# Experts of a mixture-of-experts block: inner values computed transposed, first weights stationary and fetched per tile

## The chip, the core and the metric

The kernel runs on one core of a Trainium2 chip. The time is device microseconds from start to end of one execution. The engines named below are TensorE (PE in the rows, with its weight loads listed apart as PEld), VectorE (DVE), ScalarE (ACT), GpSimd (POOL) and SyncE (SP), which here issues nearly all plain DMAs.

## What is computed

A two-layer decoder in float32 on x of shape (8, 512, 256). The change touches only the last piece, the routed feed-forward of layer 1, where each of the 4096 rows is sent to its two best of eight experts:

```python
mu = jnp.mean(x, axis=-1, keepdims=True)
var = jnp.mean(jnp.square(x - mu), axis=-1, keepdims=True)
xn = (x - mu) * jax.lax.rsqrt(var + EPS) * gamma + beta
logits = jnp.einsum('btd,ed->bte', xn, router_w)
probs = jax.nn.softmax(logits / TEMP, axis=-1)
w, idx = jax.lax.top_k(probs, K)                     # K = 2 of E = 8
wdense = jnp.sum(jax.nn.one_hot(idx, E) * w[..., None], axis=-2)
h = jax.nn.silu(jnp.einsum('btd,edf->betf', xn, W1)) # D = 256, H = 1024
y = jnp.einsum('betf,efd->betd', h, W2)
out = jnp.einsum('bte,betd->btd', wdense, y)
return out + res
```

The kernel computes only the two chosen experts of each row, not all eight.

## The kernel before

The program is a sequence of blocks, one after the other: attention and feed-forward of layer 0, attention of layer 1, cross-attention of layer 1, then `moe` (L1946), which is `route`, `experts` and `combine`. A block ends when all engines have ended their part of it.

`route` (L1971) normalises the last two batch entries, chooses their experts, and sends the normalised rows into a DRAM area `moe_sent`, grouped by expert; each send is one indirect DMA that POOL issues (`send`, L376), and POOL ends by waiting until all have arrived (L2074). Beside this SP issues the loads of all expert weights into SBUF: for each of the eight experts `w1` (256x1024, 1 MB) at L2025 and `w2` (1024x256, 1 MB) at L2026, 16 MB in all. They signal `w_in`.

`experts` (L2178) works through 72 tiles of 128 rows. Which expert a tile belongs to (`expert_of`) and where its rows start (`row_of`) are read from SBUF into registers at run time. The loops are unrolled. For a tile i the steps are:

- SP loads the rows, `xg` (L2238, two buffers), and stores the result, `y` (L2229).
- PE transposes the rows into `X` (L2254, two transposes of 128x128), ACT copies them to `xgT` (L2301).
- PE computes H = xgT.T times w1 (L2274): stationary operand xgT (two tiles of 128x128), moving operand w1 with 512 columns, two halves in two PSUM banks, 4 matmuls. The rows of the tile lie on the partitions.
- ACT applies Silu to each half and writes `h` (L2307).
- PE transposes `h` into `HT` (L2287, eight transposes), DVE copies it in two halves to `hT` (L2333), since the second product needs the 1024 inner values on the partitions.
- PE computes Y (L2262, `down`): stationary operand hT, moving operand w2 with 256 columns, 8 matmuls; DVE copies Y to `y` (L2324).

A float32 matmul that is no transpose stands in the trace as two MATMULs and two LDWEIGHTS, and a transpose as one of each. So H of a tile is 8 MATMULs of 512 columns, Y 16 of 256 columns.

The order of PE is written out by hand in `step` (L2266): H of tile i, then `down` of tile i-1, then the transposes of the rows of tile i+1, then the eight transposes of h of tile i. Waits stand in that order too: before H for `xt_done` (rows copied), before each half of the h transposes for `h_act`, before `down` for `ht_done`. PE begins the block with a wait for all of `w_in` (L2290). SP's own order in a step is: store of tile i-1, then the row load of tile i+2 (L2235 to L2238).

`combine` (L2341) gathers the two results of each row with 64 indirect DMAs from POOL (L2365), adds them on DVE and stores.

Of the kernel before, what the change touches and what calls it, by code (L numbers as in the profile page):

```python
# [21 lines left out]
P = 128  # L22
# [3 lines left out]
DT = D // P  # L26
# [1919 lines left out]
def moe(nc, sh, w, ro, out):  # L1946
# [8 lines left out]
    with ExitStack() as ctx:  # L1955
# [5 lines left out]
        with ExitStack() as inner:  # L1961
            env2 = Env(nc, inner, "ex")
            w1 = env2.sb("w1", [P, NE, DT, FH])
            w2 = env2.sb("w2", [P, NE, FT, D])
            w_in = env2.sem("w_in")
            route(nc, sh, w, ro, w1, w2, w_in, gates, expert_of, row_of, fetch)
            experts(nc, sh, w1, w2, w_in, expert_of, row_of, ro.sent, ro.results)
# [3 lines left out]
def route(nc, sh, w, ro, w1, w2, w_in, gates, expert_of, row_of, fetch):  # L1971


    with ExitStack() as ctx:
# [45 lines left out]
        def _(sp):  # L2020
# [3 lines left out]
            for e in range(NE):  # L2024
                sp.dma_start(w1[:, e], w["w1"][e].rearrange("(t p) f -> p t f", p=P)).then_inc(w_in, 16)  # L2025
# [152 lines left out]
def experts(nc, sh, w1, w2, w_in, expert_of, row_of, sent, results):  # L2178
# [5 lines left out]
    with ExitStack() as ctx:  # L2184
# [4 lines left out]
        h = sb("h", [P, FH])  # L2189
        hT = sb("hT", [P, FT, P])  # L2190
        y_sb = sb("y", [P, 2, D])
        X = env.ps("X", [P, DT, P])
        H = [env.ps(f"H{i}", [P, 512]) for i in range(2)]
        HT = [env.ps(f"HT{i}", [P, FT // 2, P]) for i in range(2)]
        Y = [env.ps(f"Y{i}", [P, D]) for i in range(2)]
        xg_in = [sem(f"xg_in{i}") for i in range(2)]
# [4 lines left out]
        ht_full = sem("ht_full")  # L2201
        ht_done = sem("ht_done")
# [20 lines left out]
        def _(sp):  # L2223
            sp.dma_start(xg[:, 0, :], tile_rows(sp, 0)).then_inc(xg_in[0], 16)
            sp.dma_start(xg[:, 1, :], tile_rows(sp, 1)).then_inc(xg_in[1], 16)
# [5 lines left out]
            def step(pair, parity, first, more):  # L2231
                i = pair * 2 + parity
                if not first:
                    store(i - 1, 1 - parity)
                if not (isinstance(i, int) and i + 2 >= TILES):  # L2235

                    sp.wait_ge(xt_full, i + 1)
                    sp.dma_start(xg[:, parity, :], tile_rows(sp, i + 2)).then_inc(xg_in[parity], 16)  # L2238

# [6 lines left out]
        def _(pe):  # L2246
# [10 lines left out]
            def down(i, parity):  # L2257
                e = expert(i)
                pe.wait_ge(ht_done, i * 2 + 2)
                pe.wait_ge(y_done, i + 1)  # L2260
                for f in range(FT):
                    mm = pe.matmul(Y[parity][:], hT[:, f, :], w2[:, bass.ds(e, 1), f, :].rearrange("p a d -> p (a d)"),  # L2262
# [3 lines left out]
            def step(pair, parity, first, more):  # L2266
                i = pair * 2 + parity
                e = expert(i)

                pe.wait_ge(xt_done, i + 1)  # L2270
                pe.wait_ge(h_act, i * 2 + 2)
                for half in range(2):
                    for dt in range(DT):
                        mm = pe.matmul(H[half][:], xgT[:, dt, :],  # L2274
# [253 lines left out]
```

## Time and profile before

| | us |
|---|---|
| median of 3 runs | 4008.63 (4007.08 to 4018.28) |
| the profiled execution, whole | 4008.86 |
| its span, first to last instruction | 4006.7 |
| `route`, about | 3247 to 3302 |
| `experts`, first row load issued to last result copied | 3303.4 to 3885.9 |
| `combine`, to the end | 3888 to 4007 |

Over the span PE is busy 83%, DVE 57%, ACT 47%, POOL 24%. Times in the rows are microseconds from the start of the span, "x8" is a count of merged instructions, and in a timeline the second column is the length of the merged piece. A PE piece ends with the pipeline of its last MATMUL, so it overlaps the next piece by about 0.2 us; the distance between the starts of two pieces is what a piece costs when PE is fed. [...]

### The profile page before, as it was taken

What the parts mean: (1) busy time and instruction counts of PE and PEld (TensorE: products, weight loads), DVE (VectorE), ACT (ScalarE), POOL (GpSimd) and SP (SyncE); (2) the same over time, 40 slices, a digit from 0 to 9 for tenths busy, and PEclk for the clock granted to TensorE, in tenths of its full rate; (3) what the DMA queues carried; (4) which work ended last, traced back from release to release, by engine and by line L of the source; (5) the groups of instructions that cost most, each with busy time, mean ns of one, the idle gap of its engine ahead of it and who ended that gap; (6) DMA issues with size and microseconds to landing.
All of it is one profiled execution on the core that took longest, in us unless ns stands there. A gap on an engine that the chain in (4) does not pass through costs nothing. (4 is left out here: it accounts for less than half of the span.)

```text
span 4006.7 us, 74067 instructions
## 1 busy us (share of the span) xinstructions
PE 3339.5 (83%) x25632; PEld 2464.7 (62%) x25632; DVE 2300.4 (57%) x7397; ACT 1893.5 (47%) x4614; POOL 953.0 (24%) x758
## 2 busy tenths in 40 slices
PE   6888888858689589898888977999999939999970
PEld 3656565547678466665666655777777736767650
DVE  4777777758867356656666553566666642222226
ACT  4787778833342165555555534555555512121210
POOL 0000000024200376776667720001111130000014
PEclk8999999977799799999999988999999969999995
DMA  3111111010200121121212211000000051111113
GB/s 107 49 50 49 55 56 67 30 29 1 97 2 1 62 57 49 51 54 49 53 49 54 54 27 54 13 13 20 23 23 23 24 207 32 32 35 34 34 42 109
DMA packets 111257, 187.56 MB, mean 47 GB/s; under 512 B 23792, under 2 KB 66224, under 8 KB 106032
## 3 DMA queue, kind: packets, MB, share of 16 engines
q1 hardware_dynamic: 100000, 131.44, 11.4%
q0 software_dynamic: 10896, 51.39, 3.4%
q8 instruction: 216, 3.54, 0.4%
q14 instruction: 145, 1.19, 0.1%
HBM read 91.93 MB, written 57.28 MB: 37 GB/s over the span
## 5 line engine op out<-in xcount | busy, mean ns | idle before, releaser
L1064 ACT ACTIVATE a_t<-a_t,a_neg 128x512 f32<-128x512 f32 (+3 forms) x1024 | 642.6, 633 | 9.1 <-DVE a_neg L1282 8.2
L891 PE MATMUL a_T<-ident,a_t 128*128 128x128 f32 x3328 | 509.6, 287 | 125.6 <-ACT a_pT L1055 56.7
L891 PEld LDWEIGHTS a_T<-ident,a_t 128*128 128x128 f32 x3328 | 382.1, 145 | 321.2 <-issue 288.3
L1055 ACT ACTIVATE a_pT<-a_T 128x512 f32<-128x512 f32 (+3 forms) x768 | 370.1, 512 | 270.8 <-PE a_T L891 270.7
L1277 DVE CUSTOM_DVE_ANT_0 a_t<-a_A,a_decay 128x512 f32<-128x512 f32 x512 | 323.0, 687 | 99.7 <-PE a_A L856 99.5
L1277 DVE CUSTOM_DVE_ANT_0 a_t<-a_A,a_table 128x384 f32<-128x384 f32 (+3 forms) x512 | 221.0, 487 | 168.1 <-PE a_A L868 166.8
L1113 POOL TENSOR_TENSOR a_rsin<-a_rawswapped,a_sin 128x512 f32<-128x512 f32 x128 | 168.4, 1316 | 557.8 <-DMA a_rawswapped<-a_raw 535.8
L2324 DVE COPY experts_y<-experts_Y 128x256 f32<-128x256 f32 x72 | 30.6, 425 | 438.2 <-PE experts_Y L2262 438.2
L2274 PE MATMUL experts_H<-ex_w,experts_xgT 128*128 x576 | 261.2, 596 | 0.9 <-ACT experts_xgT L2301 0.6
L2262 PE MATMUL experts_Y<-ex_w,experts_hT 128*128 x1152 | 260.5, 379 | 1.0 <-DVE experts_hT L2333 1.0
L2262 PEld LDWEIGHTS experts_Y<-ex_w,experts_hT 128*128 128x128 f32 x1152 | 218.8, 190 | 61.3 <-issue 35.2
L1055 ACT ACTIVATE x_pT<-x_T 128x512 f32<-128x512 f32 (+1 forms) x320 | 178.0, 592 | 163.1 <-PE x_T L891 143.3
L1277 DVE CUSTOM_DVE_ANT_0 x_t<-x_A,x_table,x_mx 128x512 f32<-128x512 f32 x256 | 177.6, 749 | 134.2 <-PE x_A L868 133.6
L2365 POOL DMA_INDIRECT combine_got<-moe_results,moe_fetch x64 | 62.2, 973 | 628.4 <-PEq L2343 593.6
L1252 DVE COPY a_pT<-a_T 128x512 f32<-128x512 f32 (+3 forms) x256 | 148.3, 579 | 94.6 <-PE a_T L891 92.8
L2307 ACT ACTIVATE experts_h<-experts_H 128x512 f32<-128x512 f32 x144 | 86.0, 597 | 240.8 <-PE experts_H L2274 240.8
L1064 ACT ACTIVATION_READ_ACCUMULATOR a_t<-a_t,a_neg 128x1 f32 x1024 | 196.5, 192 | 0.0
L1064 ACT ACTIVATE x_t<-x_t,x_neg 128x576 f32<-128x576 f32 x256 | 194.7, 765 | 0.0
L827 PE MATMUL a_A<-a_wo,a_oT 128*128 128x256 f32 x640 | 165.1, 410 | 31.3 <-DVE a_mx L1277 22.8
L912 PEld LDWEIGHTS a_O<-a_pT,a_v 128*64 128x64 f32 x2560 | 138.1, 137 | 66.1 <-ACT a_pT L1055 41.3
L868 PE MATMUL a_A<-a_khl,a_qhl 64*128 64x128 f32 (+3 forms) x1536 | 158.0, 337 | 22.9 <-POOL a_khl L1123 20.1
L1086 POOL DMA_DIRECT2D moe_sent<-a_zeros x33 | 17.6, 539 | 659.9 <-ACT a_xT L1024 659.9
(329 smaller groups left out, 6885.7 us busy)
## 6 DMA issues: line engine op xcount, KB each, us to landing
moe_sent<-a_zeros POOLq DMA_DIRECT2D x33, 1024.0 KB, 8.2
a_rawswapped<-a_raw SPq DMA_DIRECT2D x512, 64.0 KB, 2.0
a_invrep<-a_inv_dram SPq DMA_DIRECT2D x64, 256.0 KB, 3.9
ex_w<-in_f_w_dram SPq DMA_DIRECT2D x16, 1024.0 KB
experts_xg<-moe_sent SPq DMA_DIRECT2D x72, 128.0 KB, 2.0
moe_results<-experts_y SPq DMA_DIRECT2D x72, 128.0 KB, 1.7
x_invrep<-x_inv_dram SPq DMA_DIRECT2D x32, 256.0 KB, 3.9
x_all<-in_x_dram SPq DMA_DIRECT2D x1, 4096.0 KB, 14.4
```

Of the source, the lines that this page charges most:

```text
L827: mm = pe.matmul(bank[:, 0:D], oT[:, t, qt * P:(qt + 1) * P], wo[:, t, :], start=(t == 0), stop=(t == n_o - 1))
L868: mm = pe.matmul(A[seg.bank(at)][:, 0:keys(u)], q_hl[r, gp, ql, j // 2, q], k_hl[r, gp, kl_, j // 2, 0:keys(u)], start=(n == 0), stop=(n = ...
L891: mm = pe.transpose(bank[:, kt, :], t_of(u, j, kt * P, (kt + 1) * P), sh.ident[:])
L912: mm = pe.matmul(O[pr][64 * half:64 * half + 64, q], v_sb[:, kt, col], p_tile(u, j, kt), start=(kt == 0), stop=last, skip_group_check=True)
L1055: nc.scalar.activation(to, of, ACT.Copy).then_inc(t_empty, 1)
L1064: nc.scalar.activation(t_of(u_e % U, j, 0, n), t_of(u_e % U, j, 0, n), ACT.Exp, bias=neg[:, slot, j:j + 1], scale=SCALE, accum_out=total[: ...
L1113: nc.gpsimd.tensor_tensor(rsin[:], raw_swapped[:, n % 2, :], sin[:], ALU.mult).then_inc(sin_done, 1)
L1252: nc.vector.tensor_copy(p_tile(u, 3, 0, kts), bank[:, 0:kts, :] if kts > 1 else bank[:, 0, :])\
L1277: nc.vector.tensor_tensor_reduce(t_of(s, j, 0, n), A[seg.bank(name)][:, 0:n], table[:, at:at + n], 1.0, mx1[:, slot, j:j + 1] if x1 else L ...
L2262: mm = pe.matmul(Y[parity][:], hT[:, f, :], w2[:, bass.ds(e, 1), f, :].rearrange("p a d -> p (a d)"), start=(f == 0), stop=(f == FT - 1))
L2274: mm = pe.matmul(H[half][:], xgT[:, dt, :], w1[:, bass.ds(e, 1), dt, half * 512:(half + 1) * 512] .rearrange("p a f -> p (a f)"), start=(d ...
L2307: nc.scalar.activation(h[:, half * 512:(half + 1) * 512], H[half][:], ACT.Silu).then_inc(h_act, 1)
```

## The change

The first product is turned round. `w1` becomes the stationary operand, in 16 tiles of 128x128, and `xgT` with its 128 columns the moving one, so that the 1024 inner values come out on the partitions. ACT's Silu writes them straight into `hT`, which now has two buffers. The eight transposes of h, their PSUM banks and DVE's two copies are gone. H of a tile is 16 matmuls (32 MATMULs in the trace) of 128 columns.

`w1` is no longer loaded for all experts in `route`. It has two buffers, and SP fetches the 1 MB of each tile's expert in `experts` (`weights_of`), for tile i+2 after H of tile i is done; 72 such fetches. PE waits for `w1_in` before H. `w2` is still loaded whole in `route`, and PE waits for it before the first `down`. PE's order in a step is now H of tile i, the transposes of the rows of tile i+1, `down` of tile i-1. SP's order is: row load of tile i+2, weight fetch of tile i+2, store of tile i-1.

```diff
@@ -1960,15 +1960,14 @@
         fetch = env.sb("fetch", [P, GROUPS], U32)
         with ExitStack() as inner:
             env2 = Env(nc, inner, "ex")
-            w1 = env2.sb("w1", [P, NE, DT, FH])
             w2 = env2.sb("w2", [P, NE, FT, D])
             w_in = env2.sem("w_in")
-            route(nc, sh, w, ro, w1, w2, w_in, gates, expert_of, row_of, fetch)
-            experts(nc, sh, w1, w2, w_in, expert_of, row_of, ro.sent, ro.results)
+            route(nc, sh, w, ro, w2, w_in, gates, expert_of, row_of, fetch)
+            experts(nc, sh, w["w1"], w2, w_in, expert_of, row_of, ro.sent, ro.results)
         combine(nc, sh, fetch, gates, ro.results, out)
 
 
-def route(nc, sh, w, ro, w1, w2, w_in, gates, expert_of, row_of, fetch):
+def route(nc, sh, w, ro, w2, w_in, gates, expert_of, row_of, fetch):
 
 
     with ExitStack() as ctx:
@@ -2022,7 +2021,6 @@
             sp.dma_start(beta[:], w["beta"]).then_inc(loaded, 16)
             sp.dma_start(router[:], w["router_wT"].rearrange("(t p) e -> p t e", p=P)).then_inc(loaded, 16)
             for e in range(NE):
-                sp.dma_start(w1[:, e], w["w1"][e].rearrange("(t p) f -> p t f", p=P)).then_inc(w_in, 16)
                 sp.dma_start(w2[:, e], w["w2"][e].rearrange("(t p) d -> p t d", p=P)).then_inc(w_in, 16)
 
         @block.tensor
@@ -2175,7 +2173,7 @@
             steps.link(nv.tensor_tensor(gates[:], ro.packed[:, :, NE:], total[:].to_broadcast([P, BQ, TOP]), ALU.mult))
 
 
-def experts(nc, sh, w1, w2, w_in, expert_of, row_of, sent, results):
+def experts(nc, sh, w1_dram, w2, w_in, expert_of, row_of, sent, results):
 
 
 
@@ -2186,20 +2184,18 @@
         sb, sem = env.sb, env.sem
         xg = sb("xg", [P, 2, D])
         xgT = sb("xgT", [P, DT, P])
-        h = sb("h", [P, FH])
-        hT = sb("hT", [P, FT, P])
+        w1 = sb("w1", [P, 2, DT, FH])
+        hT = sb("hT", [P, 2, FT, P])
         y_sb = sb("y", [P, 2, D])
         X = env.ps("X", [P, DT, P])
-        H = [env.ps(f"H{i}", [P, 512]) for i in range(2)]
-        HT = [env.ps(f"HT{i}", [P, FT // 2, P]) for i in range(2)]
+        H = [env.ps(f"H{i}", [P, FT // 2, P]) for i in range(2)]
         Y = [env.ps(f"Y{i}", [P, D]) for i in range(2)]
+        w1_in = [sem(f"w1_in{i}") for i in range(2)]
         xg_in = [sem(f"xg_in{i}") for i in range(2)]
         xt_full = sem("xt_full")
         xt_done = sem("xt_done")
         h_full = sem("h_full")
         h_act = sem("h_act")
-        ht_full = sem("ht_full")
-        ht_done = sem("ht_done")
         y_full = sem("y_full")
         y_done = sem("y_done")
         stored = [sem(f"stored{i}") for i in range(2)]
@@ -2221,8 +2217,14 @@
 
         @block.sync
         def _(sp):
-            sp.dma_start(xg[:, 0, :], tile_rows(sp, 0)).then_inc(xg_in[0], 16)
-            sp.dma_start(xg[:, 1, :], tile_rows(sp, 1)).then_inc(xg_in[1], 16)
+            def weights_of(i, parity):
+                e = sp.value_load(expert_of[0:1, i:i + 1], min_val=0, max_val=NE - 1)
+                sp.dma_start(w1[:, parity], w1_dram[bass.ds(e, 1)].rearrange("a (t p) f -> p (a t) f", p=P))\
+                  .then_inc(w1_in[parity], 16)
+
+            for i in range(2):
+                sp.dma_start(xg[:, i, :], tile_rows(sp, i)).then_inc(xg_in[i], 16)
+                weights_of(i, i)
 
             def store(i, parity):
                 sp.wait_ge(y_done, i + 1 + 2)
@@ -2230,12 +2232,14 @@
 
             def step(pair, parity, first, more):
                 i = pair * 2 + parity
+                if i + 2 < TILES:
+
+                    sp.wait_ge(xt_full, i + 1)
+                    sp.dma_start(xg[:, parity, :], tile_rows(sp, i + 2)).then_inc(xg_in[parity], 16)
+                    sp.wait_ge(h_full, i * 2 + 2)
+                    weights_of(i + 2, parity)
                 if not first:
                     store(i - 1, 1 - parity)
-                if not (isinstance(i, int) and i + 2 >= TILES):
-
-                    sp.wait_ge(xt_full, i + 1)
-                    sp.dma_start(xg[:, parity, :], tile_rows(sp, i + 2)).then_inc(xg_in[parity], 16)
 
             steps(sp, step)
             store(TILES - 1, 1)
@@ -2256,55 +2260,52 @@
 
             def down(i, parity):
                 e = expert(i)
-                pe.wait_ge(ht_done, i * 2 + 2)
+                pe.wait_ge(h_act, i * 2 + 2)
                 pe.wait_ge(y_done, i + 1)
                 for f in range(FT):
-                    mm = pe.matmul(Y[parity][:], hT[:, f, :], w2[:, bass.ds(e, 1), f, :].rearrange("p a d -> p (a d)"),
+                    mm = pe.matmul(Y[parity][:], hT[:, parity, f, :], w2[:, bass.ds(e, 1), f, :].rearrange("p a d -> p (a d)"),
                                    start=(f == 0), stop=(f == FT - 1))
                 mm.then_inc(y_full, 1)
 
             def step(pair, parity, first, more):
                 i = pair * 2 + parity
-                e = expert(i)
-
                 pe.wait_ge(xt_done, i + 1)
-                pe.wait_ge(h_act, i * 2 + 2)
+                pe.wait_ge(w1_in[parity], pair * 16 + 16)
                 for half in range(2):
-                    for dt in range(DT):
-                        mm = pe.matmul(H[half][:], xgT[:, dt, :],
-                                       w1[:, bass.ds(e, 1), dt, half * 512:(half + 1) * 512]
-                                       .rearrange("p a f -> p (a f)"), start=(dt == 0), stop=(dt == DT - 1))
+                    if i:
+                        pe.wait_ge(h_act, i * 2 - 1 + half)
+                    for j in range(FT // 2):
+                        f = half * (FT // 2) + j
+                        for dt in range(DT):
+                            mm = pe.matmul(H[half][:, j, :], w1[:, parity, dt, f * P:(f + 1) * P], xgT[:, dt, :],
+                                           start=(dt == 0), stop=(dt == DT - 1))
                     mm.then_inc(h_full, 1)
+                if more:
+
+                    transpose_rows(1 - parity, pair + (parity + 1))
+                if i == 1:
+                    pe.wait_ge(w_in, 16 * NE)
                 if not first:
                     down(i - 1, 1 - parity)
-                if more:
-
-                    transpose_rows(1 - parity, pair + (parity + 1))
-                for half in range(2):
-                    pe.wait_ge(h_act, i * 2 + (half + 1 + 2))
-                    for j in range(FT // 2):
-                        f = half * (FT // 2) + j
-                        mm = pe.transpose(HT[half][:, j, :], h[:, f * P:(f + 1) * P], sh.ident[:])
-                    mm.then_inc(ht_full, 1)
-
-            pe.wait_ge(w_in, 16 * 2 * NE)
+
             transpose_rows(0, 1)
             steps(pe, step)
             down(TILES - 1, 1)
 
         @block.scalar
         def _(act):
-            act.sem_inc(h_act, 2)
-
             def copy_rows(i):
                 act.wait_ge(xt_full, i + 1)
                 nc.scalar.activation(xgT[:], X[:], ACT.Copy).then_inc(xt_done, 1)
 
             def step(pair, parity, first, more):
                 i = pair * 2 + parity
+                if i >= 2:
+                    act.wait_ge(y_full, i - 1)
                 for half in range(2):
                     act.wait_ge(h_full, i * 2 + (half + 1))
-                    nc.scalar.activation(h[:, half * 512:(half + 1) * 512], H[half][:], ACT.Silu).then_inc(h_act, 1)
+                    nc.scalar.activation(hT[:, parity, half * (FT // 2):(half + 1) * (FT // 2), :], H[half][:],
+                                         ACT.Silu).then_inc(h_act, 1)
                 if more:
                     copy_rows(i + 1)
 
@@ -2328,10 +2329,6 @@
                 if not first:
 
                     result(i - 1, 1 - parity, pair + parity)
-                for half in range(2):
-                    dve.wait_ge(ht_full, i * 2 + (half + 1))
-                    nc.vector.tensor_copy(hT[:, half * (FT // 2):(half + 1) * (FT // 2), :],
-                                          HT[half][:]).then_inc(ht_done, 1)
 
             steps(dve, step)
             result(TILES - 1, 1, TILES // 2)
```

How this stands in the program of PE, for one steady step in the middle of `experts`. "ISA" is register arithmetic, TENSOR_LOAD the reading of an expert's number into a register. Before, from the end of one `down`, with the X and h transposes (L2254, L2287) and the first of the four H matmuls (L2274):

```order
L2262 ISA
L2262 MATMUL experts_Y<-ex_w,experts_hT 128x256
L2254 MATMUL experts_X<-ident,experts_xg 128x128 x2
L2287 MATMUL experts_HT<-ident,experts_h 128x128 x8
L2248 TENSOR_LOAD moe_expertof
L2248 ISA x2
L2274 ISA
L2274 MATMUL experts_H<-ex_w,experts_xgT 128x512
```

And now, with H at L2280, the X transposes at L2258 and `down` at L2266:

```order
L2266 MATMUL experts_Y<-ex_w,experts_hT 128x256
L2280 MATMUL experts_H<-experts_xgT,experts_w 128x128 x16
L2258 MATMUL experts_X<-ident,experts_xg 128x128 x2
L2252 TENSOR_LOAD moe_expertof
L2252 ISA x2
L2266 ISA
L2266 MATMUL experts_Y<-ex_w,experts_hT 128x256
L2266 ISA
```

The transposes of h are gone, H has no register work left, and the reading of the expert's number stands once in a step, behind the transposes of X.

The same for SP, one steady step. Before:

```order
L2220 TENSOR_LOAD moe_rowof
L2220 ISA x2
L2238 ISA
L2238 DMA experts_xg<-moe_sent 128x256
L2229 DMA moe_results<-experts_y 128x256
```

And now, where `experts_w` is the double buffer of w1:

```order
L2216 TENSOR_LOAD moe_rowof
L2216 ISA x2
L2238 ISA
L2238 DMA experts_xg<-moe_sent 128x256
L2221 TENSOR_LOAD moe_expertof
L2221 ISA x2
L2222 ISA
L2222 DMA experts_w<-in_f_w_dram 128x2x1024
L2231 DMA moe_results<-experts_y 128x256
```

A second register load and the 1 MB fetch stand between the row load and the store.

## Rows read from the trace of the kernel before

**Rows 1.** Stage table: us, busy of each engine, PEclk, DMA share, GB/s.

```profile
3280.00:3306.00 26.00, 0.57 (x2) 0.29 (x2) 8.67 (x17) 0.00 (x0) 11.86 (x12) 0.50 0.94 349
3562.00:3626.00 64.00, 64.00 (x274) 44.94 (x273) 13.86 (x25) 12.62 (x24) 0.00 (x0) 1.00 0.11 34
```

**Rows 2.** Timeline of one steady step: start, length, engine, line, operation, idle before.

```profile
3592.52 1.04 PE L2287 MATMUL experts_HT<-ident,experts_h 128*128 128x128 f32 x8
...
3593.39 3.60 PE L2274 MATMUL experts_H<-ex_w,experts_xgT 128*128 x8
...
3596.83 3.62 PE L2262 MATMUL experts_Y<-ex_w,experts_hT 128*128 x16
...
3597.03 0.60 ACT L2307 ACTIVATE experts_h<-experts_H 128x512 f32<-128x512 f32 x1 [1.12 <-PE experts_H L2274]
...
3600.28 0.38 PE L2254 MATMUL experts_X<-ident,experts_xg 128*128 128x128 f32 x2
...
3600.70 0.39 ACT L2301 ACTIVATE experts_xgT<-experts_X 128x256 f32<-128x256 f32 x1 [3.08 <-PE experts_X L2254]
```

**Rows 3.** Timeline, start of H of tiles 1, 2 and 71.

```profile
3313.97 3.69 PE L2274 MATMUL experts_H<-ex_w,experts_xgT 128*128 x8 [0.33 <-issue]
...
3322.05 3.60 PE L2274 MATMUL experts_H<-ex_w,experts_xgT 128*128 x8
...
3872.72 3.60 PE L2274 MATMUL experts_H<-ex_w,experts_xgT 128*128 x8
```

**Rows 4.** Weight folding of layer 0 (L1694): two timeline pieces, then its stage table.

```profile
1104.60 1.95 PE L1694 MATMUL fold_C<-fold_lowdown 128*128 128x128 f32 x16
...
1117.16 3.93 PE L1694 MATMUL fold_C<-fold_chaindown,fold_lowdown 128*128 128x128 f32 x32 [2.60 <-ACT fold_chaindown L1731]
...
1094.00:1098.00 4.00, 4.00 (x36) 3.91 (x34) 1.00 1.04 429
```

**Rows 5.** Weight load of the folding, ns min/median/max; then a cross-attention piece of 64 columns.

```profile
L1694 PEld LDWEIGHTS fold_C<-fold_lowdown x16: 187/192/192, 1104.4 to 1106.2; 128*128 128x128 f32 x16
...
3000.88 1.00 PE L791 MATMUL x_A<-x_ctxT,x_wk 128*128 128x64 f32 x8
```

**Rows 6.** PE's sequencer in the step of rows 2: ns min/median/max, first to last start.

```profile
L2248 PEldq TENSOR_LOAD <-moe_expertof x1: 447/447/447, 3593.6 to 3593.6; - x1
...
L2262 PEldq FUSED_REGOPS  x8: 46/46/46, 3594.6 to 3595.5; - x8
```

**Rows 7.** End of `route`: last send, DMA table, SP's first load; then first gathers of `combine`.

```profile
3294.24 0.96 POOL L379 DMA_INDIRECT moe_sent<-moe_router,moe_place  x1 [0.30 <-issue]
...
3300.00:3302.00 2.00, 0.00 (x0) 0.00 (x0) 0.00 (x0) 0.00 (x0) 0.00 (x0) 0.50 1.10 356
...
L2220 SPq TENSOR_LOAD <-moe_rowof x72: 262/267/505, 3302.4 to 3864.8; - x72
...
3897.68 0.95 POOL L2365 DMA_INDIRECT combine_got<-moe_results,moe_fetch  x1 [0.30 <-issue]
...
3900.50 3.45 DVE L2388 SCALAR_TENSOR_TENSOR x_all<-combine_got,moe_gates,x_all 128x256 f32<-128x256 f32 x8 [12.22 <-DMA combine_got<-moe_results,moe_fetch]
```

**Rows 8.** Timeline, start of `experts`: the first two row loads and H of tile 0.

```profile
3303.39 0.37 SPq L2224 DMA_DIRECT2D experts_xg<-moe_sent  x1
3304.55 0.36 SPq L2225 DMA_DIRECT2D experts_xg<-moe_sent  x1
...
3306.69 5.61 PE L2274 MATMUL experts_H<-ex_w,experts_xgT 128*128 x8 [0.60 <-ACT experts_xgT L2301]
```

**Rows 9.** DMA issues: what, count, KB each, median us from issue to landing.

```profile
fold_down<-in_f_w_con_dram SPq DMA_DIRECT2D x1, 1024.0 KB, 5.4
...
a_wq<-in_a_w_q_dram SPq DMA_DIRECT2D x1, 1024.0 KB, 7.7
...
moe_router<-in_f_router_row_dram SPq DMA_DIRECT2D x1, 1024.0 KB, 10.2
```

**Rows 10.** Timeline, the copy of the last result.

```profile
3885.50 0.42 DVE L2324 COPY experts_y<-experts_Y 128x256 f32<-128x256 f32 x1 [3.96 <-PE experts_Y L2262]
```

## The prediction

> **What bounds the kernel now.** I read first the stage table, because the change touches only `route` and `experts`. [...]
>
> Then the timeline of one step. The reader is to take the distance from one start to the next. The h transposes start at 3592.52, H at 3593.39, Y at 3596.83, the X transposes at 3600.28 [rows 2]. That makes 0.87 us for the h transposes (8 MATMULs, 0.109 each), 3.44 for H (8, 0.430 each), 3.45 for Y (16, 0.216 each), and 0.22 for X. Sum 7.98 us. From H of tile 2 (3322.05) to H of tile 71 (3872.72) are 69 steps [rows 3], 550.67 / 69 = 7.98 each, so this step stands for all.
>
> **Part 1: H with w1 stationary.** The columns streamed stay the same: before 8 MATMULs of 512, now 32 of 128. What changes is that each 128 columns now bring a weight load of their own, 32 a tile in place of 8. The question is how fast pairs of a full 128x128 load and a 128-column MATMUL follow each other. The old step shows such pairs only as transposes (0.109 us). The nearest row with true float32 matmuls is the folding of weights in layer 0, which has exactly the new shape: 16 MATMULs in a piece of 1.95 us, of which the last one's own length is 0.275, so 15 distances in 1.675, 0.112 us each; in a window of 4 us at clock 1.00 there are 36, 0.111 each, and this with the DMA engines at a share of 1.04 [rows 4]. A second piece, 32 in 3.93, gives (3.93 - 0.275) / 31 = 0.118 [rows 4]. The cross-attention piece with 64 columns and the same full loads, 8 in 1.00, gives about (1.00 - 0.275) / 7 = 0.104 [rows 5], so the load itself can follow the load before at about 0.104, and the columns at 0.109. I take 0.112, from the piece nearest in kind, and keep 0.109 and 0.118 as ends. H of a tile becomes 32 x 0.112 = 3.58 us (3.49 to 3.78), against 3.44.
>
> [...] What the rows show: a weight load lasts 187 to 192 ns [rows 5], and still Y's 16 pairs follow each other at 0.216 us, the time of their 256 columns alone (twice 128 at 0.109), so the loads lie beside the MATMULs. [...]
>
> **Part 2: the transposes of h are gone.** 8 x 0.109 = 0.87 us of PE a tile, wholly on the path, since PE is never idle. Steady step: 3.58 + 0.22 + 3.45 = 7.25 against 7.98, 0.73 less. There are 70 steps from H of tile 1 to H of tile 71: **51.1 us** gained (57.4 with 0.109, 37.1 with 0.118).
>
> **Part 3: what PE waits for in the new order.** Silu and the row copy cost nothing before and must still do so. ACT starts the second Silu 0.2 us after H ends (3597.03 against 3596.83) for 0.60, then copies the rows for 0.39 [rows 2]; with X transposed 0.22 after H, xgT is ready about 1.3 us after H ends, and `down` of the tile before covers 3.45. The Silu result is wanted one step later. The waits for an H bank and ACT's wait for `y_full` concern work of the tile before, done by then: nothing. The sequencer: reading the expert's number begins at 3593.6 and the register work of all eight Y matmuls is done by 3595.5 [rows 6], 1.9 us in which PE lives from its queue. Now this begins when H and X are handed over, with up to 3.8 us of work queued. I cost it at nothing; if the queue held less than that, up to 1.0 us (3593.6 to 3594.6) would show in each step. H needs no register work any more, which I count as nothing too. The two DVE copies were hidden and bring nothing.
>
> **Part 4: the fetch of w1.** It adds 72 transfers of 1 MB. One is issued when SP sees H of tile i done, after a register load (about 1.0 us from the load at 3302.4 [rows 7] to the issue at 3303.39 [rows 8]). It is needed at H of tile i+2: 0.22 + 3.45 + 3.58 + 0.22 + 3.45 = 10.9 us after H of tile i ends. So 9.8 us are there for issue to landing. Rows for 1 MB: 5.4 us alone, 7.7 in a group of loads, 10.2 behind a loaded queue [rows 9]. In steady state only 1.25 MB move in 7.25 us, 180 GB/s, where `route` moved 349 [rows 1] and the folding 429 beside dense PE work [rows 4]. I take 5.5, hidden with 4 us to spare. Behind the waiting SP instructions stands the store of tile i-1; it is ready only when `down` of i-1 ends, 3.7 us after H of i, later than the fetch's issue, and its buffer is wanted two steps later. Row loads go ahead of the fetch. Nothing.
>
> **Part 5: `route` and the start.** Half of the 16 MB leaves `route`. The DMA engines are full to 3302 (share 1.10 in 3300 to 3302), while POOL issued its last send at 3294.24 + 0.96 = 3295.2; SP's first load of `experts` is at 3302.4 [rows 7]. So the arrivals waited behind the weight loads. Without w1 the 8.4 MB less at about 0.39 MB a us are 21 us of transfer, and the loads end before the sends. In `combine` the first wait ends at 3900.50, 1.9 us after the eighth gather was issued (3897.68 + 0.95) [rows 7]. By that `route` ends at 3297.1 and SP starts at 3297.2, 5.2 earlier. Then the new start: first row load 1.0 later, 3298.2; w1 of tile 0 one load and issue later (3304.55 - 3303.39 = 1.16 [rows 8]), 3299.35; landed 5.5 later, 3304.9 (up to 3307.0 with 7.7). H of tile 0 is at the low clock for its first part: before 5.61 in place of 3.60 [rows 2, 8], 2.0 more; now 3.58 + 0.2 + 2.0 = 5.8 to its end as a piece, so 3310.6. With no `down` to cover it, PE then waits for the second Silu and the row copy, 1.2 to 1.3: H of tile 1 at 3311.9 against 3313.97 [rows 3]. **2.1 us** gained (2.9 gained at best, 0.4 lost with a slow first fetch). The wait for w2 stands before the first `down`, long met.
>
> **Part 6: the end.** Before, 3872.72 [rows 3] to the last copy at 3885.50 [rows 10] are 12.78 us: H, Y, h transposes, the wait for their copies, Y. Now 3.58 + 3.45 + 3.45 + 0.4 for the last pipeline and the semaphore = 10.9. **1.9 us** gained.
>
> **Sum.** 51.1 + 2.1 + 1.9 = 55.1. Against the profiled execution (span 4006.7, whole 4008.86, which is 0.2 from the median 4008.63): 4008.9 - 55.1 = 3953.8, so 3954.
>
> **The rivals.**
> (a) *The pair runs at the transposes' 0.109*: 57.4 + 2.9 + 2.0 = 62, time 3946. [...] Against: the folding's 0.111 to 0.112.
> (b) *The pair runs at 0.118 or a few tenths a step are lost at the sequencer*: 37.1 + 1.0 + 1.7 = 40, time 3969; with the slow first fetch 3971. For it: the longer folding piece. Against: that piece stands between waits for ACT, and the long unbroken run gives 0.111.
> [...]
> (d) *The fetch sets the pace.* From 9.8 us of landing on, two steps take 3.58 + 1.1 + the landing. At the 10.2 of the worst 1 MB row this is 7.44 a step, 0.54 gained, time 3967; slower than before only from 11.3 us on. For it: SP has one queue, with loads and stores in it. Against: the bandwidth above. [...]
> (e) *Nothing gained*: only if the transposes' 0.87 had been hidden, which PE busy 64.00 of 64 us [rows 1] excludes, or by a mixture of (b) and (d).
>
> **How the numbers follow.** Forecast 0.50 (3950 to 3960), (a) 0.20, (b) 0.18, (c) 0.03, (d) 0.06, (e) 0.03. The time is the forecast's, 3954. For the range I go down to (a) with the best start, 3944, and up to (b) and the mild form of (d), 3972; outside are (c), (e) and the bad half of (d), about 0.10, which leaves something for what I did not see. A measurement of this kernel can tell 0.3%, 12 us, from no change. Faster by more than that: the forecast, (a), (b), most of (d), 0.94. Within: (e), 0.02. Slower: (c) and the bad end of (d), 0.04.
>
> **What would show it.** In the profile after: H pieces of 32 MATMULs start to start with X in about 3.58; a step of 7.25; `experts_H` at clock 1.00; w1 landing in 5 to 8 us and PE never idle for it after the first tile; route's last arrivals some 5 us earlier; DVE busy about 1.3 us less a tile. The forecast is wrong if a gap opens before H (fetch) or before Y (sequencer), or if the distance inside H is above 0.12.

## The result

| | us |
|---|---|
| predicted | 3954 (3944 to 3972) |
| measured, median of 4 | 3950.99 (3944.79 to 3955.89) |
| before, median of its runs beside it | 4007.86 |
| ratio | 0.9861, 95% interval 0.9846 to 0.9877 |
| the profiled execution, span | 3945.3 (before 4006.7) |

The change makes the kernel 57 us faster by the medians, 1.4%. The prediction said 55.

What answers to [rows 1], the stage table of the same stretch: us, busy of PE, PEld, DVE, ACT and POOL, PEclk (the granted clock, 1.00 for full), DMA share, GB/s.

```profile
3500.00:3564.00 64.00, 64.00 (x447) 60.41 (x446) 3.82 (x9) 12.60 (x26) 0.00 (x0) 1.00 0.54 185
```

PE is as full as before and at a granted clock of 1.00, but the weight loads are now busy 60.41 of 64 us (44.94 before). DVE fell from 13.86 to 3.82, the DMA share rose from 0.11 to 0.54.

The steady step, which answers to [rows 2]:

```profile
3545.49 3.73 PE L2280 MATMUL experts_H<-experts_xgT,experts_w 128*128 128x128 f32 x32
...
3549.06 0.38 PE L2258 MATMUL experts_X<-ident,experts_xg 128*128 128x128 f32 x2
...
3549.28 3.62 PE L2266 MATMUL experts_Y<-ex_w,experts_hT 128*128 x16
...
3549.75 0.38 ACT L2299 ACTIVATE experts_xgT<-experts_X 128x256 f32<-128x256 f32 x1
3549.98 0.39 SPq L2222 DMA_DIRECT2D experts_w<-in_f_w_dram  x1
...
3552.73 3.73 PE L2280 MATMUL experts_H<-experts_xgT,experts_w 128*128 128x128 f32 x32
```

From start to start H takes 3.57 us (32 pairs, 0.1116 each), X 0.22, Y 3.45, the step 7.24. None of these rows has idle time before it. ACT's row copy (3549.75) ends 2.6 us before the H that needs it.

The first and the last H, and the last result copy, which answer to [rows 3, 8, 10]:

```profile
3299.25 6.09 PE L2280 MATMUL experts_H<-experts_xgT,experts_w 128*128 128x128 f32 x32 [3.54 <-DMA experts_w<-in_f_w_dram]
...
3306.30 3.84 PE L2280 MATMUL experts_H<-experts_xgT,experts_w 128*128 128x128 f32 x32 [0.74 <-ACT experts_xgT L2299]
...
3813.55 3.73 PE L2280 MATMUL experts_H<-experts_xgT,experts_w 128*128 128x128 f32 x32
...
3824.30 0.42 DVE L2325 COPY experts_y<-experts_Y 128x256 f32<-128x256 f32 x1 [3.03 <-PE experts_Y L2266]
```

(3813.55 - 3306.30) / 70 = 7.246 a step. The fetches and their landing, which answer to [rows 9]; this row is from the page:

```profile
experts_w<-in_f_w_dram SPq DMA_DIRECT2D x72, 1024.0 KB, 4.9
```

Put together, the two profiled executions differ by 61.4 us of span, in these pieces (`route` starts with DVE's clearing of its scratch, at 3247.55 before and 3238.96 after):

| stretch | before | after | difference |
|---|---|---|---|
| start to `route` | 3247.55 | 3238.96 | -8.6 |
| `route` start to H of tile 1 | 66.42 | 67.34 | +0.9 |
| H of tile 1 to H of tile 71 | 558.75 | 507.25 | -51.5 |
| H of tile 71 to last result copy | 12.78 | 10.75 | -2.0 |
| to the end | 121.2 | 121.0 | -0.2 |

The first line is not the change's. The code there is the same, and in the ten other profiled executions of this study, nine of them of the changed kernel or of kernels built on it, `route` starts anywhere from 3236.68 to 3255.61. The last line is not either: it is `combine`, 115.6 to 120.3 in the ten others. The three lines that the change can move sum to 52.6. The interval of the ratio is 49 to 62 us and holds both this and the medians' 57; what the other 4 us are, these runs don't tell apart from the scatter.

### The profile page after: what moved, and what is told of

It is laid out like the page before. It is cut to its first block and busy times, and to the rows that moved or that the text cites. A ratio compares the mean times of both kernels' runs of the same rounds, so it can differ in the third digit from the quotient of the medians.

```text
span 3945.3 us, 76215 instructions
## 1 busy us (share of the span) xinstructions
PE 3287.6 (83%) x26784; PEld 2555.4 (65%) x26784; DVE 2202.3 (56%) x7253; ACT 1887.7 (48%) x4614; POOL 955.3 (24%) x758
## 5 line engine op out<-in xcount | busy, mean ns | idle before, releaser
L2307 ACT ACTIVATE experts_hT<-experts_H 128x512 f32<-128x512 f32 x144 | 86.0, 597 | 415.0 <-PE experts_H L2280 415.0
L2280 PEld LDWEIGHTS experts_H<-experts_xgT,experts_w 128*128 128x128 f32 x2304 | 270.7, 193 | 8.5 <-issue 3.9
L2280 PE MATMUL experts_H<-experts_xgT,experts_w 128*128 128x128 f32 x2304 | 271.3, 276 | 4.3 <-DMA experts_w<-in_f_w_dram 3.5
L2266 PE MATMUL experts_Y<-ex_w,experts_hT 128*128 x1152 | 260.4, 379 | 0.0
L2266 PEld LDWEIGHTS experts_Y<-ex_w,experts_hT 128*128 128x128 f32 x1152 | 213.3, 190 | 26.1
L2362 POOL DMA_INDIRECT combine_got<-moe_results,moe_fetch x64 | 62.3, 973 | 574.1 <-PEq L2340 539.4
```

The lines of the kernel that those rows point to most:

```text
L2266: mm = pe.matmul(Y[parity][:], hT[:, parity, f, :], w2[:, bass.ds(e, 1), f, :].rearrange("p a d -> p (a d)"), start=(f == 0), stop=(f == F ...
L2280: mm = pe.matmul(H[half][:, j, :], w1[:, parity, dt, f * P:(f + 1) * P], xgT[:, dt, :], start=(dt == 0), stop=(dt == DT - 1))
L2307: nc.scalar.activation(hT[:, parity, half * (FT // 2):(half + 1) * (FT // 2), :], H[half][:], ACT.Silu).then_inc(h_act, 1)
```

## The experiments

**The changed kernel again.**

> The changed kernel as it is, once more, for its interval and for the time at which route starts. In its first profile route starts at 3238.96, in that of before at 3247.55, though the code ahead of it is the same. Theory A (those 8.6 us differ from run to run): route starts anywhere within some 10 us here, the ratio to before stays near 0.986 to 0.987, and the part that the change moves (route start to end of the last result copy) is 585.3 us as in the first profile, within 1. Theory B (the change moves something ahead of route): route starts near 3239 again, within 2 us.

Measured 3945.98 us (6 runs), ratio 0.9851, interval 0.9824 to 0.9877.

```profile
3242.06 0.08 DVE L2077 MEMSET route_scratch<- 128x24 f32 x1 [0.64 <-PEq L502]
...
3827.42 0.42 DVE L2325 COPY experts_y<-experts_Y 128x256 f32<-128x256 f32 x1 [3.03 <-PE experts_Y L2266]
```

`route` starts 3.1 us later than in the first profile, and from there to the last result copy are 585.36 us (585.34 in the first). Theory A: the part that the change touches repeats to 0.1 us, the parts ahead of it and behind it scatter (from the last result copy to the end 116.3 us here, 121.0 in the first profile).

**The turned product alone.**

> All of w1 is loaded in route as before, and H reads w1 of expert i modulo 8 at a fixed address, so it is only the turned product and the dropped transposes; the choice of expert for the first product is left out. Theory A: the gain is the turned product's alone, step 7.25 against 7.98, 51 us for 70 steps, and the end 2.0; route start to H of tile 1 comes back to 66.2 us (after: 67.3, before: 66.4), so this kernel is 1 us faster than the change. Rival (Part 5 of the prediction, the fetch brings 2.1 us by freeing route of 8 MB): this kernel is 2 us slower than the change. Second rival: the 1 MB fetches slow PE's reads, then the step here is below 7.25.

This kernel leaves out the choice of the expert: the first product of tile i reads the w1 of expert i modulo 8, whatever expert the tile belongs to. The diffs from here on are against the changed kernel, except where another is named.

```diff
-                sp.dma_start(w1[:, parity], w1_dram[bass.ds(e, 1)].rearrange("a (t p) f -> p (a t) f", p=P))\
-                  .then_inc(w1_in[parity], 16)
...
+                sp.dma_start(w1[:, e], w["w1"][e].rearrange("(t p) f -> p t f", p=P)).then_inc(w_in, 16)
...
-                            mm = pe.matmul(H[half][:, j, :], w1[:, parity, dt, f * P:(f + 1) * P], xgT[:, dt, :],
+                            mm = pe.matmul(H[half][:, j, :], w1[:, i % NE, dt, f * P:(f + 1) * P], xgT[:, dt, :],
```

Measured 3951.3 us, ratio 0.9875 (0.9837 to 0.9912). That is 5 us above the changed kernel's second median, with `route` starting 7.4 us later in this profile, so the medians can't tell the two apart. The stretches can. PE's H of tiles 1 and 71:

```profile
3315.36 3.84 PE L2271 MATMUL experts_H<-experts_xgT,ex_w 128*128 128x128 f32 x32 [0.74 <-ACT experts_xgT L2289]
...
3822.62 3.73 PE L2271 MATMUL experts_H<-experts_xgT,ex_w 128*128 128x128 f32 x32
```

Its step is 7.247, the same as with the fetch, so the fetch neither helps nor slows PE, and the whole gain of the steps is the turned product's. `route` start (3249.49) to H of tile 1 is 65.87, 1.5 less than the changed kernel's 67.34. These 1.5 us are not the fetch's: they are there by the first send of `route` already, 27.06 us after `route` start here and 28.55 there, because of PE's clock in the router product (see Part 5). From the first send to H of tile 1 both take 38.8. So the rival of Part 5, that freeing `route` of 8 MB brings 2 us, falls. The freeing does bring something: SP's first load of `experts` comes 24.6 us after the first send in the changed kernel and 27.8 here. The wait for the first w1 then takes the 3.2 us back.

Whether the turned product could do without the fetch and still pick the right expert, no run shows.

**The fetch alone.**

> The products and transposes of before, but w1 fetched per tile into two buffers. Theory A: PE stays fed, step 7.98 within 0.01, route start to H of tile 1 67.6 us against 66.4 before; time as before within 2 us. Rival (the fetch alone brings something, as its register work goes from PE and the first load in route shrinks): over 2 us faster than before. Rival 2: it costs some tenths a step by contention, over 10 us slower than before.

Against the kernel before:

```diff
+                sp.dma_start(w1[:, parity], w1_dram[bass.ds(e, 1)].rearrange("a (t p) f -> p (a t) f", p=P))\
+                  .then_inc(w1_in[parity], 16)
...
-                                       w1[:, bass.ds(e, 1), dt, half * 512:(half + 1) * 512]
-                                       .rearrange("p a f -> p (a f)"), start=(dt == 0), stop=(dt == DT - 1))
+                                       w1[:, parity, dt, half * 512:(half + 1) * 512], start=(dt == 0), stop=(dt == DT - 1))
```

Measured 4001.12 us (10 runs), ratio 1.0001 (0.9979 to 1.0023): no difference. From one X start to the next the step is 7.98:

```profile
3563.00 0.38 PE L2261 MATMUL experts_X<-ident,experts_xg 128*128 128x128 f32 x2
...
3570.98 0.38 PE L2261 MATMUL experts_X<-ident,experts_xg 128*128 128x128 f32 x2
```

H no longer needs PE's register work here, and that too brings nothing, as the prediction counted. `route` start (3241.21) to H of tile 1 (3308.71) is 67.5, 67.6 expected.

**The order of X and down.**

> The changed kernel with the X transposes of tile i+1 put back behind down of tile i-1. Theory: nothing covers ACT's copy of the rows then: from start of X to start of H 0.42 + 0.38 + 0.05 = 0.85 in place of 0.22, so a step of 7.88, 71 x 0.63 = 45 us slower than the change, most of its gain gone. Rival: PE's queue or a faster release hides it, step 7.25 to 7.4, under 10 us slower.

```diff
-                if more:
-
-                    transpose_rows(1 - parity, pair + (parity + 1))
                 if i == 1:
                     pe.wait_ge(w_in, 16 * NE)
                 if not first:
                     down(i - 1, 1 - parity)
+                if more:
+
+                    transpose_rows(1 - parity, pair + (parity + 1))
```

Measured 4001.86 us, ratio 0.9991 (0.9974 to 1.0009): the gain is gone. The 70 steps take 51.8 us more than in the changed kernel, 45 were expected. The lines of PEld are weight loads.

```profile
3566.04 0.38 PE L2258 MATMUL experts_X<-ident,experts_xg 128*128 128x128 f32 x2
...
3566.46 0.39 ACT L2299 ACTIVATE experts_xgT<-experts_X 128x256 f32<-128x256 f32 x1 [3.08 <-PE experts_X L2258]
...
3566.89 3.65 PEld L2280 LDWEIGHTS experts_H<-experts_xgT,experts_w 128*128 128x128 f32 x32 [0.71 <-ACT experts_xgT L2299]
3566.89 3.84 PE L2280 MATMUL experts_H<-experts_xgT,experts_w 128*128 128x128 f32 x32 [0.47 <-ACT experts_xgT L2299]
3567.84 0.34 SPq L2238 DMA_DIRECT2D experts_xg<-moe_sent  x1
3569.04 0.60 ACT L2307 ACTIVATE experts_hT<-experts_H 128x512 f32<-128x512 f32 x1 [2.20 <-PE experts_H L2280]
3570.57 3.62 PE L2266 MATMUL experts_Y<-ex_w,experts_hT 128*128 x16
```

X to H is 0.85 us as expected. The step is 7.99, 0.11 more than expected, because H now takes 3.68 and not 3.57: after the wait its first weight load has nothing to hide behind, and the second MATMUL starts 0.213 us after the first, where in the changed kernel it is 0.110. That load starts together with H's first MATMUL, where in the changed kernel it starts 0.22 ahead of it (3545.49), beside the end of Y:

```profile
3545.27 3.76 PEld L2280 LDWEIGHTS experts_H<-experts_xgT,experts_w 128*128 128x128 f32 x32
```

In the kernel before the eight transposes of h, 0.87 us from start to start, covered the row copy of 0.39 [rows 2]. Taking them away needed another cover, and without the new order, with `down` behind X, nothing of the gain is left.

**Does the load or do the columns set the distance of a pair?**

> Each 128-column MATMUL of H is cut into two of 64 columns, each with its full 128x128 weight load: 64 pairs a tile in place of 32, the same columns. If the columns set the distance of a pair, H stays at 3.57 us and the step at 7.25. If the load sets it (0.104 us in the cross-attention piece of 64 columns), H is 64 x 0.104 = 6.7 and the step 10.3 us, 217 us slower than the change. If the load's own length did (0.190), H is 12.2 and the step 15.8.

```diff
-                        for dt in range(DT):
-                            mm = pe.matmul(H[half][:, j, :], w1[:, parity, dt, f * P:(f + 1) * P], xgT[:, dt, :],
-                                           start=(dt == 0), stop=(dt == DT - 1))
+                        for c in range(2):
+                            for dt in range(DT):
+                                mm = pe.matmul(H[half][:, j, c * 64:(c + 1) * 64], w1[:, parity, dt, f * P:(f + 1) * P],
+                                               xgT[:, dt, c * 64:(c + 1) * 64], start=(dt == 0), stop=(dt == DT - 1))
```

Measured 4222.8 us (one run).

```profile
3560.10 7.25 PE L2281 MATMUL experts_H<-experts_xgT,experts_w 128*128 128x64 f32 x64
...
3567.19 0.39 PE L2258 MATMUL experts_X<-ident,experts_xg 128*128 128x128 f32 x2
...
3570.87 7.25 PE L2281 MATMUL experts_H<-experts_xgT,experts_w 128*128 128x64 f32 x64
```

H is 7.09 us, 0.111 a pair although a pair has half the columns, and the step is 10.77. So something that comes once a pair sets the distance, the load or a fixed cost. It came out above the 0.104 that the expectation took from the 64-column piece [rows 5]. That 0.104 was a mean over seven distances: between the starts of that piece's single MATMULs the first distance is 0.058 and the other six are 0.111 to 0.112. The router product in `route`, with full loads and only 8 columns, says the same in the traces of before and after: 0.111 to 0.112 a pair where the granted clock is 1.00, and 0.213 to 0.215 where it is 0.50.

Next, loads of half the width, which should tell the load from a fixed cost:

> H once more, each matmul cut in both directions: weight loads of 64 columns and MATMULs of 64 columns, 128 pairs a tile in place of the 64 of the cut in columns alone, which stood 0.111 us apart. If what sets that distance is the number of columns that a load brings in, a pair of half-width loads takes about 0.056, H stays at 7.1 us and the step at 10.8, as with the cut in columns alone. If it is a fixed cost of each pair (handing over an instruction, the pipeline), H is 128 x 0.111 = 14.2 and the step 17.9 us, about 500 us longer than the cut in columns alone.

```diff
-                        for dt in range(DT):
-                            mm = pe.matmul(H[half][:, j, :], w1[:, parity, dt, f * P:(f + 1) * P], xgT[:, dt, :],
-                                           start=(dt == 0), stop=(dt == DT - 1))
+                        for s, c in ((0, 0), (0, 1), (1, 0), (1, 1)):
+                            for dt in range(DT):
+                                mm = pe.matmul(H[half][s * 64:(s + 1) * 64, j, c * 64:(c + 1) * 64],
+                                               w1[:, parity, dt, f * P + s * 64:f * P + (s + 1) * 64],
+                                               xgT[:, dt, c * 64:(c + 1) * 64], start=(dt == 0), stop=(dt == DT - 1))
```

Measured 4051.85 us (one run), faster than the cut in columns alone:

```profile
3567.31 4.99 PE L2281 MATMUL experts_H<-experts_xgT,experts_w 128*64 128x64 f32 x128
...
3572.24 0.44 PE L2258 MATMUL experts_X<-ident,experts_xg 128*128 128x128 f32 x2
```

128 pairs in 4.93 us, 0.0385 each, a step of 8.75: there is no fixed cost of 0.111, and the number of columns that a load brings in is what the 0.111 pays for. It is less even than half of 0.111, which neither expectation had. The starts of the single MATMULs say why: of eight distances in a row five are 0.052 to 0.059, about half of 0.111, and three are 0.003 to 0.006, so some pairs start beside the one before. In the next run the pairs go to the two halves of the output partitions by turns.

> Each weight tile of H is cut into two of 64 columns that go to the two halves of the output partitions by turns; the MATMULs keep 128 columns: 64 pairs a tile. If half-width pairs on the two halves of the array overlap, as the quarters' 0.0385 us a pair (below half of 0.111) suggests, a pair costs about half of 0.109, H is 64 x 0.0545 = 3.5 us and the step 7.2, up to 6 us faster than the change. If they don't overlap, the 128 columns of each MATMUL cost 0.109 each, H is 7.0 and the step 10.7, 240 us slower.

```diff
                         for dt in range(DT):
-                            mm = pe.matmul(H[half][:, j, :], w1[:, parity, dt, f * P:(f + 1) * P], xgT[:, dt, :],
-                                           start=(dt == 0), stop=(dt == DT - 1))
+                            for s in range(2):
+                                mm = pe.matmul(H[half][s * 64:(s + 1) * 64, j, :],
+                                               w1[:, parity, dt, f * P + s * 64:f * P + (s + 1) * 64],
+                                               xgT[:, dt, :], start=(dt == 0), stop=(dt == DT - 1))
```

Measured 3963.6 us, ratio 0.9879 (0.9846 to 0.9912).

```profile
3562.05 3.71 PE L2281 MATMUL experts_H<-experts_xgT,experts_w 128*64 128x128 f32 x64
...
3565.69 0.44 PE L2258 MATMUL experts_X<-ident,experts_xg 128*128 128x128 f32 x2
...
3565.97 3.62 PE L2266 MATMUL experts_Y<-ex_w,experts_hT 128*128 x16
...
3569.52 3.71 PE L2281 MATMUL experts_H<-experts_xgT,experts_w 128*64 128x128 f32 x64
```

64 pairs in 3.64 us, 0.057 each, where a MATMUL of 128 columns in the transposes takes 0.109 [rows 2]: here half-width pairs that go to the two halves of the output partitions run beside each other. Their MATMULs start two by two, 0.006 to 0.007 apart, and the next two 0.109 later. But H is not shorter than 3.57, and X and Y around it are longer by 0.16 a step (X 0.28, Y 3.55), where full and half width follow each other. The step is 7.47 and not the 7.2 expected, 15.7 us more in 70 steps than in the changed kernel. No gain.

**How much room the fetch has.**

> A second, unused 1 MB is fetched ahead of each w1, and PE waits for both. Landing of w1 about 8.2 us, under the 9.8 that the order leaves, and 2.36 MB in 7.25 us are under the 0.39 MB a us seen in route. Theory: step stays 7.25. Rival (the fetch is already near setting the pace): step over 7.3.

> Two unused MB are fetched ahead of each w1. Theory by the chain of waits alone: landing 10.8, step (3.57 + 1.1 + 10.8) / 2 = 7.7. Theory by bandwidth: 3.4 MB a step at 0.39 MB a us make 8.7 us. Either shows where the fetch begins to set the pace; PE then idles and the granted clock may fall.

```diff
+                sp.dma_start(extra[:, parity], w1_dram[0:2].rearrange("a (t p) f -> p (a t) f", p=P))\
+                  .then_inc(extra_in[parity], 16)
```

(0:1 for 2 MB. `extra` is a buffer that nothing reads.) Measured 3946.06 and 4055.5 us (one run each). The stage tables, first of 2 MB, then of 3 MB:

```profile
3500.00:3564.00 64.00, 64.00 (x441) 60.28 (x441) 3.82 (x9) 12.67 (x27) 0.00 (x0) 1.00 0.90 325
```

```profile
3400.00:3900.00 500.00, 427.04 (x2856) 385.22 (x2856) 24.22 (x57) 83.70 (x171) 0.00 (x0) 1.00 1.02 390
```

At 2 MB a tile and a DMA share of 0.90 PE is still full, the step 7.25 and the landing of w1 7.7 us. At 3 MB the step is 8.74 (H of tile 1 at 3312.76, of tile 71 at 3924.49), just the 3.4 MB a step at 390 GB/s: bandwidth sets it, not the chain of waits, and the landing grows to 12.2. Even there the clock stays at 1.00. The change's own fetch of 1 MB is at half of what fits.

**The first two fetches earlier.**

> The changed kernel with the first two w1 fetches moved into route, right after the experts' numbers are known there. Theory: PE no longer waits for them at the start of experts: H of tile 0 starts about 0.7 us after X, 3.5 us earlier, and route start to H of tile 1 is 64 us against 67.3: 3 us faster than the change, about 0.1%. Rival: the two fetches delay the last sends of route by as much, no gain.

```diff
+            sp.wait_ge(ro.placed, FIRST + 2)
+            for i in range(2):
+                e = sp.value_load(expert_of[0:1, i:i + 1], min_val=0, max_val=NE - 1)
+                sp.dma_start(w1[:, i], w["w1"][bass.ds(e, 1)].rearrange("a (t p) f -> p (a t) f", p=P))\
+                  .then_inc(w1_in[i], 16)
...
+            nv.tensor_copy(expert_of[:], row[:, 0]).then_inc(ro.placed, 1)
```

Measured 3945.5 us, ratio 0.9848 (0.9821 to 0.9875).

```profile
3303.80 5.93 PE L2284 MATMUL experts_H<-experts_xgT,ex_w 128*128 128x128 f32 x32 [0.47 <-ACT experts_xgT L2303]
```

The 3.54 us wait for the first w1 is gone, and from `route` start (3248.37) to H of tile 1 (3310.70) are 62.3 us, 5.0 less than in the changed kernel; 1.5 of them are the clock's (Part 5 below), 3.5 the fetch's. The rival, that the two fetches delay the sends, falls: from the first send to the end of the last it is 20.6 us, as in the kernel before (20.6) and the changed one (20.7). By the medians it can't be told from the change, whose second measurement is 3945.98.

## Why the prediction was right, and where not

**The bound** (PE in the steady part, DVE and ACT free): right. PE is busy 64.00 of 64 us at a granted clock of 1.00 before [rows 1] and after, and DVE's 10 us less in 64 brought nothing.

**Part 1**, 0.112 us a pair from the folding of layer 0: measured 0.1116, H 3.57 against 3.58. The folding, with the same operands' shapes, the same two MATMULs to a product and a DMA share of 1.04 in its long run [rows 4], was the right one to take. The longer folding piece's 0.118 (rival b) was a mean over three longer distances, one at its start and two in its middle (0.184, 0.162, 0.184); all its others are 0.111 to 0.112. The columns-only rate of 0.109 (rival a) is not reached, because the load takes 0.111, as with 64 columns. The rate of the load alone was put at 0.104, too low by 7%, because it was a mean with one short distance in it. So the load and not the columns sets the distance. It does so at 0.111; that loads follow each other at the 0.19 of their own row, as rival (c) had it, no run shows. H came out right to 0.01 us because the piece taken is itself bound by its loads; the prediction held the load to be faster than the columns.

Each load of H is 0.192 us long by its own row, and the pairs still follow each other at 0.1116, so the loads lie beside the MATMULs and beside each other. How fast loads of 64 columns can follow each other these runs don't tell: the quarters' 0.052 to 0.059 is about half of 0.111, but 64 of a MATMUL's columns, half of 0.109, would give about the same.

**Part 2**, 0.73 a step: measured 7.982 less 7.246 = 0.736, in 70 steps 51.5 against 51.1.

**Part 3**, no new wait: right for ACT and the sequencer, no row in the step has idle time. The cover that it named (`down` over the row copy) is real and worth 0.74 us a step, shown by putting X last.

**Part 4**, hidden fetch: right. Landing 4.9 us for the 5.5 taken, with 9.8 of room, and 2 MB still fit.

**Part 5** is the step that failed: 2.1 us gained was forecast, 0.9 lost was measured. Three terms. The first is the end of `route`. After the last send is issued, `experts` began 7.2 us later before, and was to begin 2.0 later; it begins 3.9 later, which leaves 3.3 us gained of the 5.2 forecast:

```profile
3287.21 0.97 POOL L379 DMA_INDIRECT moe_sent<-moe_router,moe_place  x1 [0.30 <-issue]
...
3290.00:3291.00 1.00, 0.00 (x0) 0.00 (x0) 0.00 (x0) 0.00 (x0) 0.00 (x0) 0.50 0.00 0
...
3293.08 0.37 SPq L2226 DMA_DIRECT2D experts_xg<-moe_sent  x1
```

SP's register load stands 1.0 before its DMA, at 3292.1. Of the 2.0, 1.9 was read at gathers that wait for nothing else, and was carried over to stores into DRAM with a block's end behind them. DMA engines are at rest from 3290 on, so 2 us pass in which nothing is moved; which part of that is the arrival of the last store's signal and which the change of blocks, these runs don't tell. The second term is PE's clock inside `route`, for which the prediction had no term: the small router product ran in 4.05 us before and 6.84 after. The stage tables of a stretch inside it, first before, then after, have the granted clock at 1.00 and at 0.50:

```profile
3260.00:3262.00 2.00, 2.00 (x21) 2.00 (x20) 0.00 (x0) 1.28 (x2) 1.86 (x2) 1.00 1.03 410
...
3252.00:3254.00 2.00, 2.00 (x11) 2.00 (x11) 0.00 (x0) 0.71 (x2) 1.86 (x2) 0.50 1.06 387
...
3251.48 6.84 PE L2039 MATMUL route_R<-route_router,route_xnT 128*128 128x8 f32 x32
```

The code there is the same, and the short length occurs without w1's loads in `route` too (about 4 in before, in the turned product alone, in the 3 MB fetch and in `early`; 6.8 in the eight others), so the change does not set it alone; whether it makes the long one likelier, twelve profiles don't tell. The short one starts the sends 1.5 us sooner (27.0 us after `route` start, against 28.5). The third term, the wait for the first w1, was right: 14.2 us from SP's first register load to H of tile 1, 14.7 forecast. H of tile 0 does begin at a low granted clock, 0.50 in 3306 to 3310 before and 0.50 in 3300 to 3302 after. Together 1.9 and 1.5 lost and 0.5 won make the 3.0 between the 2.1 forecast and the -0.9 measured, within 0.1.

**Part 6**: 2.0 for 1.9. The 0.4 for the last pipeline and the semaphore was the author's estimate; 10.75 less 3.57 and twice 3.45 leaves 0.28.

So the forecast of 55 stood on the 70 steps and the end, 53.0 of it, and 53.5 were measured there. The other 2 were wrong and are hidden in the scatter ahead of `route`, whose start lies within 19 us over the twelve profiles. That the median comes within 3 us of the forecast is partly luck: the stretch that the change touches gained 52.6. Of the rivals (c), (d) and (e) none occurs; (d) starts between 2 and 3 MB a tile.

## What to carry to other kernels

Where PE is the bound and a result has to be transposed for the next product, compute it transposed: swap stationary and moving operand, and the transposes and their copies go, as long as the new moving operand has enough columns to cover a load. In float32 at 128 columns it all but does (0.1116 us a pair, 0.109 for the columns by the transposes), at 64 it doesn't (0.111 for half the columns). When work is taken out of a queue, ask what it covered: here the removed transposes hid a copy of 0.4 us, and without the new order the whole gain was gone. And price an edit at the nearest piece of the same trace that has its shapes; the estimate taken from another kind of transfer was the one that failed. Look at the single distances in such a piece before dividing its length by their number: both the 0.104 and the 0.118 were means over one or a few odd distances among many of 0.111 to 0.112.

## What the runs showed of the hardware

- A full 128x128 float32 load costs 0.111 to 0.112 us in a run of pairs at a granted clock of 1.00, with 8 (router product before), 64 (cut in columns) or 128 moving columns (H of the changed kernel) alike, though each load is 0.19 long by its own row. At a granted clock of 0.50 (router product, 8 columns) it is 0.213 to 0.215.
- Half-width pairs that go to the two halves of the output partitions overlap: by turns 0.057 us a pair with 128 moving columns, with starts 0.006 to 0.007 apart, and 0.0385 in the cut in both directions with 64.
- After the wait for the row copy, with X last, H of 32 pairs takes 0.11 us more than in a running queue (3.68 against 3.57).
- With 2 MB a tile, DMA at 0.90 share (325 GB/s) beside PE at 64.00 of 64 us cost PE nothing (step 7.25); with 3 MB, at a share of 1.02 (390 GB/s), the transfers set the step, 8.74.
- 1 MB fetched from SP's queue lands in 4.9 us (median of 72) in the changed kernel, in 7.7 with another 1 MB issued just before it.
